# A kernel of two adaLN layers: a second value buffer and moved score products in attention, and a new order of the steps that prepare the next sequence of a recurrence

## The reference

```python
# layer 0, attention: decaying linear attention with 8 heads of 16
S = g * S + k_t[..., :, None] * v_t[..., None, :]
y_t = einsum('bhde,bhd->bhe', S, q_t)
out = (out - mean) * rsqrt(var + EPS)        # over time and head, per head group
x = x + ga * (out * gn_weight + gn_bias) @ Wo.T

# layer 1, a selective state space recurrence, 256 channels, 16 states
x_s, z, B_s, C_s, dt = split(x @ W_in.T)
x_s = silu(causal_conv4(x_s) + conv_b)
dt = softplus(dt @ W_dt.T + b_dt)
h = exp(dt * A) * h + dt * B * x_s            # along time
y = (einsum('bdn,bn->bd', h, C) + x_s * D) * silu(z)
out = layer_norm(residual + y @ W_out.T)
```

## Time and profile before

| | us |
|---|---|
| median of 3 runs | 1457.13 (1445.59 to 1464.18) |
| the profiled execution's own time | 1469.19 |
| its span, first to last instruction | 1467.0 |
| busy: TensorE, VectorE, ScalarE, GpSimd | 1130.1, 893.7, 687.8, 561.8 |
| attention, 23 to 245 us | 222.0 |
| recurrence, first scan to last `yz`, 514.60 to 1005.47 us | 490.9 |

### The profile page before, as it was taken

One profiled execution on the slowest core, in us unless ns is written; L12 is line 12 of the kernel. 1 busy time (PEld: TensorE's weight loads), 2 busy tenths in 40 slices (PEclk: granted clock), 3 DMA queues, 4 the chain that ended last, 5 costly groups with the idle time before them and its releaser, 6 DMA issues. The chain is left out here.

```text
span 1467.0 us, 23954 instructions
## 1 busy us (share of the span) xinstructions
PE 1130.1 (77%) x6776; PEld 857.3 (58%) x6777; DVE 893.7 (61%) x1786; ACT 687.8 (47%) x1527; POOL 561.8 (38%) x882
## 2 busy tenths in 40 slices
PE   2887885689978688888888888883374799999860
PEld 1555554334448578777888877773243666666640
DVE  2355553711039599999999999993376633333327
ACT  1334432233324587888778887771241033333320
POOL 1000000300012277777877778770000155555540
PEclk9667775799989789999999999996555599999995
DMA  6000000011010200000000000002310011111115
GB/s 181 0 1 1 0 1 1 0 44 43 29 29 0 58 1 1 1 0 0 0 0 0 0 0 0 0 0 90 97 33 17 6 35 39 36 39 38 38 48 181
DMA packets 41607, 39.87 MB, mean 27 GB/s; under 512 B 4041, under 2 KB 37474, under 8 KB 41202
## 3 DMA queue, kind: packets, MB, share of 16 engines
q1 hardware_dynamic: 32466, 22.37, 5.2%
q0 software_dynamic: 4608, 9.45, 2.3%
q10 hardware_dynamic: 4496, 7.60, 1.5%
HBM read 30.44 MB, written 8.96 MB: 27 GB/s over the span
## 5 line engine op out<-in xcount | busy, mean ns | idle before, releaser
L1181 DVE TENSOR_TENSOR_SCAN s_hs<-s_dA,bank 128x1024 f32<-128x1024 f32 x128 | 291.9, 2280 | 10.2 <-PE bank L1532 10.1
L1409 POOL TENSOR_SCALAR s_dbuT<-s_dtuT,s_BT 128x256 f32<-128x256 f32 x512 | 239.9, 492 | 11.0 <-ACT s_dtuT L1264 8.8
L1292 ACT ACTIVATE s_dA<-s_dt,aneg 128x255 f32<-128x255 f32 x512 | 213.6, 498 | 0.6 <-DVE s_hs L1181 0.4
L1982 POOL DMA_INDIRECT x_xg<-hf_rows,x_src x72 | 69.7, 968 | 236.9 <-issue 170.6
L1532 PE MATMUL bank<-const,s_dbuT 128*128 128x128 f32 x1024 | 139.7, 282 | 26.0 <-POOL s_dbuT L1409 26.0
L1189 DVE TENSOR_TENSOR s_hc<-s_hs,bank 128x1024 f32<-128x1024 f32 x128 | 156.1, 1220 | 5.2 <-PE bank L1520 0.9
L2022 PE MATMUL bank<-w,x_xT 128*128 x288 | 128.4, 569 | 19.0 <-ACT x_xT L2064 16.3
L1550 PE MATMUL bank<-const,s_hc 128*128 128x128 f32 x1024 | 138.0, 280 | 2.2 <-DVE s_hc L1189 2.2
L1532 PEld LDWEIGHTS bank<-const,s_dbuT 128*128 128x128 f32 x1024 | 119.8, 145 | 32.7 <-issue 26.3
L1550 PEld LDWEIGHTS bank<-const,s_hc 128*128 128x128 f32 x1024 | 120.7, 145 | 2.4 <-DVE s_hc L1189 2.4
L2060 ACT ACTIVATE x_a<-bank 128x448 f32<-128x448 f32 x72 | 39.1, 543 | 161.6 <-PE bank L2022 156.7
(11 more groups left out here) (301 smaller groups left out, 2273.6 us busy)
## 6 DMA issues: line engine op xcount, KB each, us to landing
w<-in_w SPq DMA_DIRECT2D x16, 256.0 KB, 3.1
o_yr<-y_rows SPq DMA_DIRECT2D x8, 512.0 KB, 3.9
w<-in_w ACTq DMA_DIRECT2D x1, 3584.0 KB, 13.3
x_res<-in_x SPq DMA_DIRECT2D x4, 512.0 KB
gate<-gates_d SPq DMA_DIRECT2D x2, 1024.0 KB, 5.6
s_gate<-gates_d SPq DMA_DIRECT2D x2, 1024.0 KB, 7.4
hf_rows<-r_rows SPq DMA_DIRECT2D x8, 256.0 KB, 2.2
out<-o_o ACTq DMA_DIRECT2D x8, 256.0 KB, 2.4
```

What stands on the lines that cost most here:

```text
L1181: dve.tensor_tensor_scan(flat(hs[:, j % 2]), flat(dA[:, j % RING]), bDbu[j % 2], 0.0, ALU.mult, ALU.add).then_inc(S["scanned"], 1)
L1292: ins = act.activation(dA[:, j % RING, h, n, 1:], dt[:, k, h, 1:], ACT.Exp, scale=m.aneg[:, h, 2 * j + n:2 * j + n + 1])
L1409: ins = pool.tensor_scalar(dbuT[:, j % RING, c, n, :], dtuT[:, k, c, :], BT[:, k, c, 2 * j + n:2 * j + n + 1], 1.0, ALU.mult, ALU.mult)
L1982: pool.indirect_dma_start(xg[k][:], None, m.hf_rows[:, :], bass.IndirectOffsetOnAxis(ap=src[k][:, 0:1], axis=0)).then_inc(S["rows"][k], 16)
```

## The change

In attention `vp` gets a second buffer, chosen by the parity of the round; ScalarE waits for the result products of the pair two before. On TensorE the second half of the scores moves ahead of keys and queries. In the recurrence, step 2 of the preparation (dt product and softplus) is called in j = 1 instead of j = 2, step 1 on TensorE at the end of j = 0; ScalarE's steps 4 and 5 (silu, `dtuT`) come ahead of that step's decays; the convolution is split, half h = 0 in j = 3, half h = 1 in j = 4 ahead of z; on TensorE `finish` comes ahead of the preparation; the skip products (`dskip`, L1544) move from the sums of step 0 to those of step 1.

```diff
-        vp = sb("vp", [P, 2, Q, D])
+        vp = sb("vp", [P, 2, 2, Q, D])
...
-            def values(n):
+            def values(n, w):
...
-                if later(n):
-                    act.wait_ge(S["y_ps"], n)
+                if not (isinstance(n, int) and n < 2):
+                    act.wait_ge(S["y_ps"], n - 1)
...
-                if n1 is not None:
-                    keys_and_queries(n1)
                 if n2 is not None:
                     scores(n2, 1, odd)
                 if n1 is not None:
+                    keys_and_queries(n1)
                     values(n1)
...
             def body(b, k, first, prepares):
                 for j in range(SCAN_J):
+                    if prepares and j in (4, 5):
+                        prepare(j, b + 1, 1 - k)
                     if j + AHEAD < SCAN_J:
                         decays(b, k, j + AHEAD, not (first and j + AHEAD < RING))
                     elif prepares:
                         decays(b + 1, 1 - k, j + AHEAD - SCAN_J, True)
-                    if prepares and j != 2:
-                        prepare(j, b + 1, 1 - k)
+                    if prepares and j == 0:
+                        prepare(0, b + 1, 1 - k)
+                        prepare(0.5, b + 1, 1 - k)
+                    if prepares and j == 1:
+                        prepare(1, b + 1, 1 - k)
+                        prepare(2, b + 1, 1 - k)
                     if not first:
                         finish(j, b - 1, 1 - k)
-                    if prepares and j == 0:
-                        prepare(0.5, b + 1, 1 - k)
-                    if prepares and j == 2:
-                        prepare(j, b + 1, 1 - k)
...
-                if step == 3:
+                if step in (3, 3.5):
...
-                    for h in range(NH):
+                    for h in range(NH)[:1] if step == 3 else range(NH)[1:]:
...
-                if j == 0:
+                if j == 0 and not first:
+                    pe.wait_ge(S["yz"], b)
+                if j == 1:
                     pe.wait_ge(S["u_ready"], 2 * b + 2)
-                    if not first:
-                        pe.wait_ge(S["yz"], b)
...
-                    if prepares:
-                        prepare(j, b + 1, 1 - k)
+                    if prepares and j == 0:
+                        prepare(0, b + 1, 1 - k)
                     if not first:
                         finish(j, b - 1, 1 - k, prepares)
+                    if prepares:
+                        for step in {0: (1,), 1: (2,), 3: (3,), 4: (3.5, 4), 5: (5,)}.get(j, ()):
+                            prepare(step, b + 1, 1 - k)
```

More of the change, by code:

```diff
@@ L523, in values @@
                     .then_inc(S["v_sb"], 1)
-                if later(n):
-                    act.wait_ge(S["y_ps"], n)
+                if not (isinstance(n, int) and n < 2):
+                    act.wait_ge(S["y_ps"], n - 1)
                 heads = lambda t: t.rearrange("p (g a d) -> p g a d", a=2, d=DH)
                 for k in range(2):
-                    act.activation(heads(vp[:, k].rearrange("p q d -> p (q d)"))[:, :, k, :],
+                    act.activation(heads(vp[:, w, k].rearrange("p q d -> p (q d)"))[:, :, k, :],
                                    heads(bP[:, :])[:, :, k, :], ACT.Copy).then_inc(S["v_sb"], 1)
@@ L587, in body @@
                 if n1 is not None:
-                    values(n1)
+                    values(n1, 1 - odd)
                 if n0 is not None:
@@ L696, in result @@
                             mm = pe.matmul(bY[32 * j:32 * j + 32, k * L + c * P:k * L + (c + 1) * P],
-                                           vp[:, par, k * NCH + c, 32 * j:32 * j + 32],
+                                           vp[:, w, par, k * NCH + c, 32 * j:32 * j + 32],
                                            prob[:, k, j, 2 * c + par, :], start=(c == 0 and par == 0),
@@ L1476, in prepare @@
                                            hT[:, k, tap:tap + L], start=(tap == 0), stop=(tap == KCONV - 1))
-                    mm.then_inc(S["xs_ps"], 1)
+                    if step == 3.5:
+                        mm.then_inc(S["xs_ps"], 1)
                 if step == 4:
@@ L1544, in sum_states @@
                             pe.matmul(part(c, h), u[:, k, h, c * P:(c + 1) * P], m.dskip[:, h, :],
-                                      start=(c == 0 and h == 0), stop=False, skip_group_check=True)
+                                      start=False, stop=False, skip_group_check=True)
                 pe.wait_ge(S["hc_ready"], 8 * b + j + 1)
@@ L1550, in sum_states @@
                             mm = pe.matmul(part(c, h), hc[:, j % 2, h, n, c * P:(c + 1) * P], ident,
-                                           is_transpose=True, start=False,
+                                           is_transpose=True, start=(j == 0 and n == 0 and c == 0 and h == 0),
                                            stop=(j == SCAN_J - 1 and n == 1), skip_group_check=True)
@@ L1574, in last @@
                     finish(j, b, k, False)
-            for j in range(SCAN_J):
-                prepare(j, 0, 0)
+            for step in (0, 1, 2, 3, 3.5, 4, 5):
+                prepare(step, 0, 0)
             turn_inputs(0, 0, 0, True)
```

## The result

The changed kernel takes 1464.13 us (median of 14 runs, 1462.48 to 1466.38), the kernel before on the same chip 1456.8 us (14 runs, 1445.59 to 1467.77). The ratio is **1.006**, 95% interval 1.0038 to 1.0081: 7.3 us slower between the medians, which by themselves stand at 1.005. The loss is small, but the interval excludes 1.000, and 1457 was forecast. The profiled execution took 1466.02 us, 3 us less than that of before (1469.19). So the two profiles say "faster" and the medians say "slower": the changed kernel was profiled in an execution 1.9 us above its median, the kernel before in one 12.4 us above its own. Most of this study is about that.

What follows compares the result with a forecast made beforehand. No engine was full in attention; VectorE bound the recurrence. Attention +1.7 and recurrence -15.0 + 15.0 - 2.4 = -2.4 summed to -0.7 us on 1469.19, 1456 on the median, taken as 1457, range 1438 to 1478.

Steps and rivals of the forecast that it cites:

- the clock of attention: Attention: mean clock 0.74 taken as the high level for 48% of the time, weighting each round's +2.1 or -0.2 us.
- the last step: Whole kernel: -0.7 us on the profiled 1469.19, 12 us over the median, carried to 1456 on the median, taken as 1457.
- three signs named for being wrong: Profile after: `oshift` does not wait, `yz` still does, or the logits run without a wait.
- The `xn` waits: Attention, TensorE: with the second `vp` buffer seven waits of 2.2 us for `xn` go.
- `h2T`: five waits: Attention, five rounds: logits newly wait for `h2T`, covered by values alone, +2.8 us at 2.4 GHz, +1.8 at 1.2 GHz.
- The masks: Attention, moved scores: the fourth product waits longer for its mask, +1.5 us a round at 2.4 GHz, +0.2 at 1.2 GHz.
- The waits before `yz` and the scan: Recurrence, VectorE: earlier `dbuT` removes waits of 13.4 and 1.6 us, -15.0; -9.5 if 0.37 us stay per sequence.
- `oshift` waits: Recurrence, VectorE: softplus ahead delays `orstd`, a new wait of 0.9 to 1.0 us per sequence, +15.0 over fifteen.
- `least`: Recurrence: `least` no longer meets GpSimd's `dbuT` products, 0.16 x 15 = -2.4 us or nothing; by the skill's rule up to -7.
- the moves do nothing for `u`: Recurrence: convolution ends too late, `u` no earlier than 720.5, waits before `yz` stay and the new one comes; 1471, chance 0.14.
- the `oshift` wait is larger: Recurrence: TensorE reaches the dt product 2 us later, `oshift` waits 3 us, +45 in place of +15; 1487, chance 0.07.
- Both repairs pay fully: `orstd` in time, recurrence -17; masks and `h2T` covered; together -43, 1414; with half of attention's, 1427; chance 0.07.

Runs made afterwards that it cites:

- `h2T` early: The changed kernel with ScalarE writing `h2T` ahead of keys and queries instead of behind them: 1439.4 us, ratio 0.9875 to the kernel before.
- `orstd` early: The changed kernel with `olnv` and `orstd` on ScalarE ahead of the four decays of step 2: 1449.6 us, ratio 0.9961 to the kernel before.

## Why the prediction was wrong, and where it was right

**The step that failed** is the clock of attention: "The mean clock of 0.74 is the high level for 48% of the time", used as a given for both kernels, and with it the last step, "-0.7 us on the profiled execution's 1469.19, which stands 12 us over the median of three runs. On the median that is 1456". The sum let each edit change waits and nothing else, and carried a difference from one execution to the median. Both halves were wrong. In the recurrence the prediction let the low clock go together with TensorE's waits; in attention it did not. There the clock answers to the waits too: it is 0.73 to 0.82 in the seven rounds of the old code, 0.91 with the buffer alone, 0.70 with the moved scores alone, idle products in the waits lift it, and the busy time of the same 872 or 873 records runs from 99.7 to 136.2 us. And the profiled execution of before was one with a long attention (155.8 us for the rounds, where a typical one has 144.6); the changed attention has 150.6 to 154.2 us in three profiles, and its runs are narrow (4 us between the lowest and the highest, against 22). On the profiled pair the kernel gained 3 us, near the -0.7 of the sum. On the medians it lost 7.3; between the typical execution of the old attention and the changed one the rounds' busy time is +9.6 us and their idle time -3.6. None of the three signs named for being wrong came true: all three watch waits, and the waits were right.

**Attention, term by term**; right in size but for the masks:
- The `xn` waits: -15.4 forecast, 33.0 to 19.2, so -13.8. ScalarE's wait before `vp` went altogether.
- `h2T`: five waits of 1.8 to 2.8, or about 11.5 us; measured 4.7 in two before, 16.2 in seven after. The shown one has 2.28, behind values of 1.65 us, which lie between the 1.16 of the high clock (2.8 worked out) and the 2.0 of the low one (1.8).
- The masks: the wait of the fourth product at the low clock was put at 1.0 and is 0.76; with +1.5 at the high clock the term made 5.8 us over seven rounds, and the sum of all mask waits did not rise (15.1 to 14.8). This term was too large by some 6 us here, which hid a part of the clock's. With `h2T` early, where the clock is higher, the masks' sum is 17.3.
- Rounds' idle time: -1.5 us in the profiled pair, -3.6 against the typical execution, in place of +1.7.

**Right in the recurrence**, nearly to the term:
- The waits before `yz` and the scan were to give 15.0 and gave 12.3: those before `yz` went from 13.4 to 2.7, of which 2.06 are the last sequence's in both kernels, those before the scan from 1.6 to nothing, TensorE's for `dbuT` from 23.2 to 0.8, and the sequences of 31.8 us with a lower clock are gone. `u` starts at 716.54, 17.8 us after `yz` of its sequence; it was 19.1 before (719.64 - 700.55), so it is 1.3 us earlier, where 1.8 were worked out.
- Softplus starts 6.7 us after the scan's end (698.58 to 705.32), 6.6 were laid out. `oshift` waits 0.8 us, 15 times, and takes 0.22 longer: 1.0 a sequence, as the 0.9 to 1.0 forecast, though half of that precision is luck, for the second part was not foreseen.
- `least` from 0.844 to 0.660 us: 15 times 0.18 is -2.8, forecast -2.4. The Trainium skill ("SBUF — State Buffer", Who interferes with whom) has the later of two such operations blocked until the first has finished. No `least` lost a whole product of 0.46 us; 0.22 is the most that any lost. One of the slow ones, 0.88 us, started at 715.51, 0.14 us behind the first of four `dbuT` products (715.37), so the trace agrees with a wait for what was left of one product at most, and a whole one each time (-7) was too much.
- The sum was -2.4; the profile shows -3.6, the medians -2.1 with an interval that holds zero.

**The rivals.** That the moves do nothing for `u` is out: it is 1.3 us earlier. That the `oshift` wait is larger, 3 us, is out: it is 0.8. "Both repairs pay fully" was dropped for two reasons, `h2T` and `orstd` in ScalarE's queue, and each is confirmed by its removal from the changed kernel, -1.85 points and -1.0. Both removed at once was not run; by these two it would be near 0.978, some 1424 us at the 1456.8 of the first chip, at the weaker form of this rival (1427) and not at its 1414. With the scores in their old place and `orstd` early the kernel comes to 0.9687 (1411 us there), and with `h2T` early as well to 0.9626 (1402); below 1414, whose sum had no term for the clock.

**Not settled.** Why the same attention code is granted 0.91 in one execution and 0.79 in another (these two ran on different chips, but the old code had 0.73 and 0.82 on one and the same). The sum of the idle time does not set it: the change itself takes 3.6 us of idle time out of the rounds (30.9 to 27.3) and the clock falls from 0.82 to 0.76. The clock of a round doesn't follow from that round's idle share either: in the first profile of before the round from 88.64 to 116.36 us idles 4.1 of 27.7 us at a clock of 0.62, that from 141.26 to 165.10 idles 6.0 of 23.8 at 0.86. The Trainium skill ("TensorE: Matmul & The Clock Gate", the part on the clock gate) ties the clock to how busy TensorE has been lately, and the idle products agree with the direction; which waits tip it, no run here resolves. Of the 1% that the moved scores cost beside `h2T`, the share of the masks wasn't measured by itself; filling that wait with products was not tried.

## What to carry to other kernels

Where TensorE's clock is below 1.00 in a stretch, do not take it as a given. Here 14 us of idle time gone were 30 us, and 12 added were 27, so price a wait with the busy time of the same instructions at either level as well. Nor does the sum of the waits decide: old ones out and new ones in left 3.6 us less idle time and a slower kernel. Take a second execution before a sum is carried to a median; where the runs spread by more than the expected change, ask which stretch makes the spread. And two repairs in one change hide each other: the buffer and the earlier steps of the recurrence were each good, and each was eaten by one place in ScalarE's queue (`h2T`, `orstd`) that an edit of a few lines frees.

## What was not expected of the hardware

- Idle products made a kernel faster: 48 of them on TensorE, 0.81% (9.2 us between the medians, 1437.9 and 1428.7).
- An operation of two elements on VectorE, `oshift`, takes 0.134 us alone and 0.357 at the median while GpSimd is in the four `dbuT` products (710.05 to 711.89). It has nothing to do with its wait: without the wait it takes 0.33 us, beside GpSimd products of 707.48 to 709.33 in that run (`orstd` early). `least`, with 256 times the elements, loses the same 0.22 us at most.
- One attention code with nearly the same idle time (16.5 and 14.3 us) differs by 13.6 us over seven rounds between two executions, by the granted clock.
